# Value products ahead of the scores in each attention step of a transformer block kernel

## The reference

```python
q = einsum('bse,hed->bhsd', x, Wq) + bq          # k and v alike
scores = einsum('bhsd,bhtd->bhst', q, k) / sqrt(64)
scores = where(causal, scores, -inf)
out = einsum('bhst,bhtd->bhsd', softmax(scores), v)
x = layernorm(x + out.reshape(...) @ Wo + bo)
xn = layernorm(x) * gamma + beta
w, idx = top_k(softmax(xn @ router_w.T / 1.5), 2)
y = silu(xn @ W1[e]) @ W2[e]                     # for the two chosen experts
x = layernorm(x + sum of w * y)
```

## Time and profile before

| | |
|---|---|
| median of 3 runs | 1322.31 us (1321.48 to 1324.12) |
| profiled execution | 1320.37 us, its span 1318.2 us |
| busy: PE, PEld | 98%, 87% |
| busy: DVE, ACT, POOL | 84%, 82%, 38% |
| mean granted clock of TensorE | 0.996 of full speed |

### The profile page before, as it was taken

The page is one execution under the profiler, slowest core; times in us unless marked ns, Lnnn a source line. Parts: engine busy times, 40 slices in busy tenths (PEclk is TensorE's granted clock), DMA queues, the critical chain, the costliest instruction groups (busy, mean ns, idle before and its releaser), DMA issues.

```text
span 1318.2 us, 36163 instructions
## 1 busy us (share of the span) xinstructions
PE 1288.0 (98%) x11298; PEld 1141.5 (87%) x11298; DVE 1102.1 (84%) x5209; ACT 1078.2 (82%) x3481; POOL 498.7 (38%) x1067
## 2 busy tenths in 40 slices
PE   7999999999999999999999999999998999999997
PEld 6888888888888888888888888888887999999983
DVE  6888888888888888888888888888886898888856
ACT  7888888888888888888888888888885777777737
POOL 1013333333333333333333333333333675665645
PEclk9999999999999999999999999999998999999999
DMA  5011000000000000000000000000033587777748
GB/s 211 35 67 46 14 14 17 15 18 16 16 14 14 14 14 13 14 14 14 14 14 14 14 18 16 19 16 14 14 140 92 158 239 233 236 226 233 222 137 329
DMA packets 58860, 98.19 MB, mean 74 GB/s; under 512 B 9376, under 2 KB 36131, under 8 KB 58416
## 3 DMA queue, kind: packets, MB, share of 16 engines
q1 hardware_dynamic: 49024, 78.67, 19.2%
q0 software_dynamic: 8640, 17.13, 3.8%
q10 hardware_dynamic: 1008, 0.08, 0.1%
HBM read 65.85 MB, written 30.91 MB: 73 GB/s over the span
## 4 chain that ended last, share of the span: by engine, by line
PE 86%; ACT 6%; DVE 4%; issue 1%; DMA 1%; POOL 0%; ACTq 0%; SPq 0%; POOLq 0%; DVEq 0%
PE ps_f L1102 15%; PE ps_b L1136 13%; PE ps_a L1102 13%; PE ps_s L1143 12%; PE ps_s L1124 9%; PE ps_s L1102 7%; PE ps_a L1327 4%; PE ps_b L1327 4%; PE ps_s L1127 4%; ACT probs L596 2%; PE ps_s L1398 2%; ACT probs L598 2%; PE ps_a L1299 1%; PE ps_s L1148 1%; PE ps_f L1168 1%
## 5 line engine op out<-in xcount | busy, mean ns | idle before, releaser
L596 ACT ACTIVATE probs<-probs,neg_max 128x256 f32<-128x256 f32 x512 | 255.3, 499 | 134.7 <-DVE neg_max L845 134.7
L472 POOL TENSOR_SCALAR ln_b<-mv 128x2 f32<-128x2 f32 x32 | 6.1, 190 | 633.7 <-DVE mv L908 633.7
L841 DVE CUSTOM_DVE_ANT_0 probs<-ps_s,mask 128x256 f32<-128x256 f32 x512 | 214.2, 418 | 29.4 <-PE ps_s L1127 26.9
L1143 PE MATMUL ps_s<-ident,probs 128*128 128x128 f32 x1536 | 200.6, 274 | 0.9 <-issue 0.8
L1136 PE MATMUL ps_b<-pt,f_y 128*64 128x256 f32 (+1 forms) x2048 | 196.9, 334 | 3.5 <-ACT f_y L591 1.6
L598 ACT ACTIVATE probs<-probs,neg_max 128x128 f32<-128x128 f32 x512 | 198.7, 388 | 0.0
L855 DVE TENSOR_SCALAR probs<-probs,inv_sums 128x256 f32<-128x256 f32 x512 | 181.9, 355 | 9.1
L1136 PEld LDWEIGHTS ps_b<-pt,f_y 128*64 128x64 f32 x2048 | 132.6, 137 | 54.4 <-issue 9.6
L562 POOL DMA_INDIRECT y_tok<-f_y,m_dest x142 | 145.8, 1027 | 83.7 <-DVE m_dest L1008 57.2
L1124 PE MATMUL ps_s<-qk 64*128 64x256 f32 x1024 | 170.7, 409 | 5.3 <-ACT pt L631 3.0
L1143 PEld LDWEIGHTS ps_s<-ident,probs 128*128 128x128 f32 x1536 | 173.0, 143 | 1.6 <-issue 1.5
(11 more groups left out here) (205 smaller groups left out, 3144.4 us busy)
## 6 DMA issues: line engine op xcount, KB each, us to landing
m_w<-w_split SPq DMA_DIRECT2D x71, 512.0 KB
m_x<-queue SPq DMA_DIRECT2D x71, 133.0 KB
f_y<-y_tok SPq DMA_DIRECT2D x32, 256.0 KB, 6.6
queue<-empty SPq DMA_DIRECT2D x8, 532.0 KB, 4.8
x_raw<-in_x SPq DMA_DIRECT2D x32, 128.0 KB, 2.1
w_split<-f_y SPq DMA_DIRECT2D x8, 512.0 KB, 3.2
out_x<-f_y SPq DMA_DIRECT2D x16, 256.0 KB, 6.4
y_tok<-f_y,m_dest POOLq DMA_INDIRECT x142
```

Source lines behind the costliest of these rows:

```text
L596: act.activation(row[:, 0:2 * P], row[:, 0:2 * P], ACT.Exp, scale=-1.0, bias=neg_max[:, pair, h, 0:1], accum_out=sums[:, d % 2, pair, h, 0:1])
L841: dve.tensor_tensor_reduce(out=row[:, 0:2 * P], in0=ps_s[:, pair, h, 0:2 * P], in1=mask[:].rearrange("p a b -> p (a b)"), scale=-1.0, scal ...
L1143: ins = pe.transpose(ps_s[:, pair, h, dst:dst + P], probs[:, buf, pair, h, src:src + P], ident[:])
```

## The change

In TensorE's `step`, the block that waits for and issues the value products of two steps ago is moved from behind the block of the scores to in front of it. Both blocks are unchanged in themselves, with all their waits; the fillers, projections and transposes follow as before. Steps 0 and 1 have no value products, so steps 2 to 127 are the ones with a new order. The last two groups of value products, which the code issues after the loop, stay where they were.

```diff
             def step(n, q, d):
-                if d < LAST:
-                    for pair in range(2):
-                        pe.wait_ge(qk_done, d * 2 + pair + 1)
-                        if d >= 2:
-                            pe.wait_ge((pt_first_done, pt_second_done)[pair], d - 1)
-                        if pair == 1 and q == 1 and n in LATE:
-                            pe.wait_ge(r_diff_done, n - 1)
-                        if pair == 1 and q == 3 and n in LATE:
-                            pe.wait_ge(ranks_done, n - 1)
-                        scores(pair)
                 if 2 <= d < LAST + 2:
                     pe.wait_ge(pt_first_done, d - 1)
                     pe.wait_ge(pt_second_done, d - 1)
...
                     for pair in range(2):
                         ins = attention_output((d - 2) % QUADS * 2 + pair, pair)
                     ins.then_inc(o_ready, 1)
+                if d < LAST:
+                    for pair in range(2):
+                        pe.wait_ge(qk_done, d * 2 + pair + 1)
+                        if d >= 2:
+                            pe.wait_ge((pt_first_done, pt_second_done)[pair], d - 1)
+                        if pair == 1 and q == 1 and n in LATE:
+                            pe.wait_ge(r_diff_done, n - 1)
+                        if pair == 1 and q == 3 and n in LATE:
+                            pe.wait_ge(ranks_done, n - 1)
+                        scores(pair)
                 first_filler(n, q)
```

## The result

The changed kernel takes 1587.9 us (median of 4 runs, 1584.8 to 1595.7) against 1321.9 for the kernel before (4 runs). The ratio is 1.202, 95% interval 1.198 to 1.206: 266 us slower, in the forecast range of 1540 to 1605 and 13 us above its centre. The profiled execution took 1584.76 us, of which the span is 1582.6.

What follows compares the result with a forecast made beforehand. TensorE bound attention at 7.76 us a step; the new order would make a ring through the vector and scalar engines the bound. 27.8 + 1230 + 314.0 = 1571.8 us span, with time outside it 1575; range 1540 to 1605.

Steps and rivals of the forecast that it cites:

- the ring: Attention steps: products, scores, masks, exponentials, normalisation, second copy, next products form a closed loop; 9.84 us a step instead of 7.76.
- The start: Step 2, the first changed step: its mask starts at 25.14 + 2.68 = 27.82 us.
- The 125 steps: From step 2's mask to step 127's: 125 steps of 9.84 us, 1230 us.
- the release after the vector engine's copy: From the end of the second copy (line 941) to the first value product: 0.26 us.
- the link from mask to release: From mask start to what releases the next products: 6.46, 7.19, 7.16 and 7.82 us by q, 28.63 a sequence.
- The clock: TensorE in attention: busy 79% with gaps of 2.1 us in 9.84, so the sum takes 2.4 GHz throughout.
- The price for such a step: An attention step at the lower clock: 0.80 us more for products and 0.53 for scores, 1.33 us.
- The idle time: TensorE in attention: about 2.1 us idle a step, its largest wait for line 941, 200 us in all.
- The covered wait: Rival: the copy ends before TensorE needs it, same time or 1318 us at best; within 0.2% 3 in 100, faster 2.
- The partly closed ring: Rival: the ring closes but part of it shortens, through shorter waits or earlier scores; 1500 to 1540 us, 8 in 100.
- The falling clock: Rival: lower clock in many attention steps; 1659 us if in half, some 1850 if in all; 7 in 100.
- the high end of the range: 1605 us: one step in eight at the lower clock (21 us) and 0.1 us more a release, less some overlap.

Runs made afterwards that it cites:

- the last run above: Kernel before, old order, with W1's rounding and splitting spread to one piece a sequence over eight sequences: 1314.5 us, ratio 0.995 to the kernel before.
- the three kernels traced there: Against the kernel before: new order at q 2 alone, 1.038; changed kernel with second copy ahead of pair 1's normalisation, 1.108; that with first copy early too, 1.089.

## Why the prediction was right, and where it was off

The mechanism was the one forecast: the ring. That the centre came so close was partly luck, as two errors cancelled. The terms, in the order of the sum:

- *The start.* Step 2's mask begins at 28.95 (27.82 forecast), step 127's at 1268.93; the rest of the span is 313.7 us (314.0). The 1.13 us at the start aren't the order's: step 0's mask, which has no products ahead of it, was already 1.27 us later than before (12.54 against 11.27). In the timeline of the changed kernel:

```profile
28.95 0.42 DVE L841 CUSTOM_DVE_ANT_0 probs<-ps_s,mask 128x256 f32<-128x256 f32 x1 [2.52 <-PE ps_s L1127]
...
1268.93 0.42 DVE L841 CUSTOM_DVE_ANT_0 probs<-ps_s,mask 128x256 f32<-128x256 f32 x1 [1.29 <-PE ps_s L1127]
```

- *The 125 steps.* 1240.0 us, forecast 1230. By q the undisturbed steps are 8.94, 9.72, 9.69 and 10.53 us against 9.14, 9.87, 9.84 and 10.50. The one mis-sized link is the release after the vector engine's copy: 0.10 us, not the 0.26 of the earlier trace rows. That row was the only one for this copy, at the end of the stage; why it was longer there is open. Three times 0.16 is the whole 0.47 us a sequence, 15 us in all (the link from mask to release was 0.04 us shorter than summed at q 0 and 0.03 longer at q 3). At q 3 the V evacuation was last, as forecast, and its release 0.25 us.
- *The clock.* I took 2.4 GHz throughout in the sum, and that step failed. 31.25 sequences of 38.88 us are 1215 us; the other 25 are the clock, 5 us in the first three sequences and 1 in the last two. 19 us stand in the long steps after q 1 of the later sequences (17 of 28, 0.8 to 1.6 us each), and the run with spare matmuls takes them out. The row that I leaned on (76% busy between 12 and 20 us at a clock of 1.00) was one lucky sample. Its idle time was a single stretch of 1.94 us, which ended at 16.18, about as long as the 2.0 us at q 1 of the changed kernel. All 14 traces have that stretch (1.91 to 1.94 us), in a step that none of the edits touches; in six of them the clock fell to 0.50 at its end or up to 1.7 us later, and in the other eight it didn't. The trace of the last run above shows the same 6.06 us of busy TensorE at a lower clock:

```profile
12.00:20.00 8.00, 6.06 (x34) 4.68 (x32) 6.21 (x30) 6.24 (x23) 0.00 (x0) 0.79 1.01 432
```

So one row without a fall didn't show that such a stretch is safe. From the fourth sequence to the last but one the clock fell only after the longest idle stretch of a sequence, 2.0 us at q 1, behind the output projection; those of 1.0, 1.1 and 1.7 us at the other steps never came just before a fall. The passage of "TensorE: Matmul & The Clock Gate", section "A second HAM failure mode: psum-queue depth-cycling", on short idles between groups of matmuls, in the Trainium skill, was the better guide: the clock did swing, in about one step in seven. The price for such a step, 1.33 us, was near the mean of 19.4 / 17 = 1.14.
- *The cancelling.* The two errors had opposite signs, +25 and −15, which is why the 125 steps were off by only 10 us. With the late start the profiled execution was 11 us above its forecast of 1574; the median of the runs was another 3 us above the profiled execution, of which I had allowed 1.
- *The idle time.* Forecast 2.1 us a step; the waits ahead of the products are 185 us over 125 steps, 1.5, and another 0.3 stands ahead of transposes and the like. I had named the vector engine's copy as what TensorE's waits would show. It was the releaser, but the table of waits puts its time down to the scalar engine's copy or to "issue".
- *The rivals.* The covered wait needed a mask-to-copy time under 5.08 us; it is 6.42 at q 0. The partly closed ring (1500 to 1540) didn't come about. The falling clock came in part, at a seventh of the steps, which the high end of the range had priced at an eighth.

## What to carry to other kernels

Before moving a block forward in a saturated queue, write down the loop through the other engines in which its inputs are made, and add it up link by link: what counts is whether the moved block and its wait close that loop, and not how busy each engine is. A block that an engine must run anyway costs its full length again if the consumers of what it displaces are in the loop. And a copy that is already late without costing anything, here by 0.36 us, is a warning that the loop has no slack. A row in which nothing bad happened is one sample: before a term such as the clock is put at nothing on it, look at the same place in more than one execution.

## What the runs showed of the hardware

- The delay from the end of the last releasing instruction to the first waiting matmul differed by engine and place: 0.05 us after the scalar engine's copy, 0.10 after the vector engine's, 0.25 after the V evacuation, 0.15 for scores behind the copy.
- TensorE's clock went to 1.2 GHz after the idle stretch of 2.0 us at q 1, in 17 and 18 of 28 like places; with six matmuls in that stretch, in none. After the stretches of 1.7 us at q 3 of the same sequences it never did, in any of seven traces. After the stretch of 1.9 us in the first step, ahead of a V projection, it did in 6 of 14 traces.
- One of the chips ran the expert stage at 184 GB/s instead of 228 and the kernel before in 1419 us instead of 1322. In the three kernels traced there, eight of the twelve kinds of attention step were as long as elsewhere. Ratios from it understated the loss each time: 1.038 against 1.044, 1.108 against 1.134 and 1.089 against 1.112 for the same kernels.
